# An index beyond the table for edges outside a step's block, and a bound on every row gather of a graph network

## The reference

```python
def gatv2_layer(x, src, dst, Wl, bl, Wr, br, att, bias):
    xl = x @ Wl + bl
    xr = x @ Wr + br
    xj = xl[src]                                   # gather one row per edge
    e = leaky_relu(xj + xr[dst], 0.2)
    logits = e @ att
    ex = exp(logits - segment_max(logits, dst)[dst])
    alpha = ex / (segment_sum(ex, dst)[dst] + 1e-16)
    return segment_sum(alpha[:, None] * xj, dst) + bias
```

## Time and profile before

| | us |
|---|---|
| two runs of the kernel | 12,944.22 and 12,955.25, median 12,949.74 |
| span of the profiled execution, first to last instruction | 12,943.7 |
| pass E0, first to last gather | 218.2 to 2346.9 |
| pass E1 | 2449.5 to 4561.3 |
| layer 1's scatters | 4729.7 to 7807.8 |
| pass E2 | 8067.2 to 10181.7 |
| pass E3 | 10512.2 to 12723.2 |

### The profile page before, as it was taken

How to read it: one execution, slowest core, us unless ns; L and a number is a source line. 1 busy time by engine, 2 the same in 40 slices (tenths; PEclk the granted TensorE clock), 3 DMA queues, 4 the chain that set the end, 5 groups by cost and what they waited for, 6 DMA issues and landing times.

```text
span 12943.7 us, 281524 instructions
## 1 busy us (share of the span) xinstructions
PE 10725.3 (83%) x62317; PEld 8649.8 (67%) x62317; DVE 7913.5 (61%) x29130; ACT 5610.6 (43%) x14105; POOL 9352.2 (72%) x8593
## 2 busy tenths in 40 slices
PE   5788887788888878888888886999999878888886
PEld 4666666666666666666666665777777656666664
DVE  7666666666666655555555555333333568888887
ACT  1555555455555553333333335344444543333334
POOL 3777777577777758888888885777777447777775
PEclk7999999899999966666666667555555688889887
DMA  3222222422222224444444445222222222222222
GB/s 96 56 55 55 55 55 55 132 65 56 56 56 56 55 42 39 39 39 39 39 39 39 38 39 131 57 56 56 56 56 56 58 65 62 62 61 63 61 61 61
DMA packets 809108, 749.26 MB, mean 58 GB/s; under 512 B 264686, under 2 KB 691175, under 8 KB 808255
## 3 DMA queue, kind: packets, MB, share of 16 engines
q0 software_dynamic: 453440, 550.05, 24.5%
q1 hardware_dynamic: 354814, 191.38, 5.7%
HBM read 548.62 MB, written 192.13 MB: 57 GB/s over the span
## 4 chain that ended last, share of the span: by engine, by line
PE 52%; issue 9%; DVE 8%; DMA 6%; POOL 2%; ACT 2%; DVEq 2%; SPq 0%; POOLq 0%; ACTq 0%
PE bank L721 13%; PE bank L705 7%; PE bank L708 6%; DMA scatter_s<-dst_side 6%; PE bank L706 5%; PE bank L1181 4%; PE bank L1187 3%; PE bank L730 3%; PE bank L690 2%; PE bank L1196 2%; POOL scatter_s L1148 2%; DVE agg L929 1%; DVE dst_side L1274 1%; DVE lrelu L884 1%; PE bank L1190 1%
## 5 line engine op out<-in xcount | busy, mean ns | idle before, releaser
L1148 POOL DMA_INDIRECT scatter_s<-dst_side x1664 | 2566.9, 1543 | 555.4 <-DMA scatter_s<-dst_side 240.1
L808 ACT ACTIVATE oh_e<-bank,weight,minus_w 128x128 f32<-128x128 f32 x4992 | 1876.2, 456 | 1465.3 <-PE bank L730 1385.3
L920 DVE SCALAR_TENSOR_TENSOR agg<-agg,rescale,bank 128x130 f32 x4992 | 1680.8, 337 | 1211.0 <-PE bank L721 958.6
L706 PE MATMUL bank<-rows,ident 128*128 128x128 f32 x9984 | 2108.6, 296 | 0.0
L672 POOL DMA_INDIRECT rows<-gather_c,edge_sb x1664 | 1631.9, 981 | 599.6 <-issue 382.3
L672 POOL DMA_INDIRECT rows<-gather_b,edge_sb x1664 | 1605.9, 965 | 608.5 <-issue 314.8
L672 POOL DMA_INDIRECT rows<-gather_a,edge_sb x1664 | 1622.8, 975 | 555.4 <-issue 315.5
L672 POOL DMA_INDIRECT rows<-gather_s,edge_sb x1664 | 1570.3, 944 | 571.3 <-issue 378.7
L721 PE MATMUL bank<-rows,oh_e 128*128 128x130 f32 x9984 | 1873.4, 343 | 54.1 <-DVE agg L920 37.1
L721 PEld LDWEIGHTS bank<-rows,oh_e 128*128 128x128 f32 x9984 | 1601.6, 242 | 268.5 <-issue 230.4
L706 PEld LDWEIGHTS bank<-rows,ident 128*128 128x128 f32 x9984 | 1695.0, 213 | 0.0
(11 more groups left out here) (345 smaller groups left out, 19310.3 us busy)
## 6 DMA issues: line engine op xcount, KB each, us to landing
rows<-gather_a,edge_sb POOLq DMA_INDIRECT x1664
rows<-gather_b,edge_sb POOLq DMA_INDIRECT x1664
scatter_s<-dst_side POOLq DMA_INDIRECT x1664, 3.4
rows<-gather_s,edge_sb POOLq DMA_INDIRECT x1664
rows<-gather_c,edge_sb POOLq DMA_INDIRECT x1664
rows<-scatter_s SPq DMA_DIRECT2D x56, 455.0 KB, 6.1
scatter_s<-zeros SPq DMA_DIRECT2D x64, 390.0 KB, 5.7
edge_sb<-edge_tab SPq DMA_DIRECT2D x520, 40.0 KB
```

Of the source, the lines that this page charges most:

```text
L706: e.matmul(o, ident[:, :], rows[:, it.slot(), g, 0:P], start=False, stop=True).then_inc(L.side.sem, 1)
L808: e.activation(oh_e[:, g % 8, :], bank[7][:, (g % CH) * P:(g % CH + 1) * P], ACT.Relu, bias=weight[:, it.slot(2, 2), g:g + 1], scale=minus ...
L920: e.scalar_tensor_tensor(old, old, rescale[:, it.slot(2, 2), g:g + 1], sum_bank(g)[:, (g % 2) * AW:(g % 2) * AW + L.aw], ALU.mult, ALU.add ...
L1148: e.indirect_dma_start(scatter_s[k], bass.IndirectOffsetOnAxis(ap=S_.target[:, it.slot(1), g:g + 1], axis=0), S_.summed[:, g % 8, :], None ...
```

## The change

In the preparation, part(0) is no longer a copy of the source index. It is computed last, from the mask and the float index: where the mask is -1e30, 2^24 is added to the index. All four gather passes hand each gather a bound of NB * P - 1 = 12,543 in a register; a row whose index is above the bound is not fetched, and its partition keeps what was in it. So that the first use of each slot holds no arbitrary bits, the first pass also sets the 128 columns of all rows to zero before it opens.

```diff
+OUTSIDE = float(1 << 24)
...
 def dve_prep_tile(e, c):
...
             w.wait_ge(tile_turned.at(c))
-            own.did(e.tensor_copy(part(0).bitcast(I32), ps(1)))
             own.did(e.tensor_copy(part(1), ps(0)))
...
             w.wait_ge(own.so_far())
-            e.tensor_tensor(part(2), part(2), mt, ALU.add).then_inc(edges_made.sem, 1)
+            own.did(e.tensor_tensor(part(2), part(2), mt, ALU.add))
+            w.wait_ge(own.so_far())
+            e.scalar_tensor_tensor(part(0).bitcast(I32), part(2), -OUTSIDE / -NEG, part(3), ALU.mult, ALU.add).then_inc(edges_made.sem, 1)
...
 def pool_edges(e, L):
...
                         e.indirect_dma_start(rows[:, u, g, 0:L.width], None, L.src_rows,
-                                             bass.IndirectOffsetOnAxis(ap=edge_sb[:, u, g:g + 1].bitcast(I32), axis=0)
-                                             ).then_inc(L.gat[c].sem(it), 16)
+                                             bass.IndirectOffsetOnAxis(ap=edge_sb[:, u, g:g + 1].bitcast(I32), axis=0),
+                                             bounds_check=NB * P - 1, oob_is_err=False).then_inc(L.gat[c].sem(it), 16)
...
 def dve_edges(e, L):
...
             e.memset(rows[:, :, :, P:XW], 1.0)
+            if L.first:
+                e.memset(rows[:, :, :, 0:P], 0.0)
...
+        E0.first = True
```

More of the change, by code:

```diff
@@ L624, in __init__ @@
                 self.masked = one("masked")
-                self.zeroing, self.zeroed = [], None
+                self.zeroing, self.zeroed, self.first = [], None, False
             def w_last(self, it, lag, c):
```

## The result

The changed kernel takes 13,385.4 us (median of 13,412.93 and 13,357.87) against 12,949.74: a ratio of 1.0338, 95% interval 1.0319 to 1.0358. The forecast was 13,067 us, +0.9%. The sign was right, the size was off by a factor of nearly four (436 us against 117), and the time lies inside the range. The profiled execution is the one of 13,412.93 us, with a span of 13,409.9 us; 466.2 us more than the span before.

What follows compares the result with a forecast made beforehand. POOL's gather issue was taken to bound E0 and E1, nearly E2 and E3. Onto 12,949.74 us came 99.8 (E0, E1), 11 (E2), 0 (E3), 5.2 (memset) and 1.4 (preparation): 117, giving 13,067 us; range 12,770 to 14,100.

Steps and rivals of the forecast that it cites:

- What bounds the kernel: First two gather passes (E0, E1): bound by POOL's back-to-back issue; the other two (E2, E3) nearly so.
- The slack of E2, 39 us: Third gather pass: POOL's waits for PE would absorb 39 of 49.9 us, leaving 11 us.
- that of E3, 73 us: Fourth gather pass: POOL's waits on the chain through VectorE would absorb all 49.9 us, leaving 0.
- The skip saves nothing on the path: All gather passes: skipping 12,416 of 212,992 rows saves nothing in transfers; rival with skip saved: 12,773 us, chance 0.14.
- The end of the bounds at 92 us a pass: POOL's gathers: most the skip could save, if all of 0.944 us scaled with rows.
- I take x = +0.03 us: Every gather on POOL: bound's price net of the skip, chosen between -0.055 and +0.598 us; forecast's chance 0.36.
- row-by-row rival: POOL, all four passes: check paid per row, 1.2 ns each, x = 0.15, 13,843 us; chance 0.32.
- unless a gather itself takes longer: POOL's timeline in the first gather pass: starts 1.25 us apart (0.944 + 0.306), with this one exception.
- The small terms: First pass's memset, 6.9 us with 1.7 covered: +5.2 us; preparation's extra wait, 13 times 0.11 us: 1.4 us.
- The granted clock: Rival on TensorE: slower POOL idles PE, clock falls for half of three passes, 13,940 us; chance 0.08.
- the estimate of 1.28 us per gather: POOL's check at about 12 cycles per element, 1.2 GHz: some 21,400 us in all; no chance given.
- the forecast of 12,957 us: All gathers: bound costs nothing, only +7 us of small terms remains; rival "nothing moves", chance 0.10.

Runs made afterwards that it cites:

- c3: Changed kernel without the bound, no index outside the table, each gather fetching 64 rows instead of 128: 15,217.67 us, single run, against 15,201.85 for the kernel before.
- a3: Changed kernel with the bound set to 0, so nearly every row is skipped: 15,141.35 us, single run, 0.6% over the kernel before.
- b4: Changed kernel with the bound on the third gather pass (E2) alone and no index outside the table: 13,020.07 us, 1.0048 of the kernel before.
- b1: The changed kernel again, unedited, on a chip like the first: 13,429.66 us, 1.0364 of the kernel before.
- a1: Changed kernel with the bound on all gathers but every index inside the table, so no row is skipped: 15,304.99 us against 15,054.77, 1.0156.
- c4: Changed kernel with the bound, no index outside the table, each gather fetching 64 rows instead of 128: 15,262.52 us, single run, against 15,201.85 for the kernel before.
- b2: Changed kernel without the VectorE multiplication by att (L888): 13,106.56 us, 1.0116 of the kernel before.
- b3: Kernel before the change, without the VectorE multiplication by att: 12,839.76 us, 0.9912 of the kernel before.
- a4: Changed kernel with the VectorE multiplication by att (L888) replaced by one with a constant, one SBUF input: 15,265.9 us, 1.0134 of the kernel before.
- c1: Kernel before the change, with the leaky relu's maximum kept in PSUM and multiplied by att from there: 0.9974 of the kernel before.
- a2: Changed kernel without the bound and with no index outside, leaving the memset and the later index: 15,068.54 us, 1.0013 of the kernel before.

## Why the prediction was right in sign and wrong in size

- **What bounds the kernel.** Right. E0 and E1 grew by what their gathers grew, 140.3 and 148.0 us of busy time for 140.6 and 148.4 us of pass. The slack of E2, 39 us, was 37.8; that of E3, 73 us, gave only 43.4, and 30 us of waits stayed. The forecast counts all slack as cover, 112 us; 81 were.
- **The skip saves nothing on the path.** The forecast took it as nothing; that held more strictly than argued. The end of the bounds at 92 us a pass was far out: even rows that are left out altogether save 0.7 ns each (c3), and skipped ones save none (a3; b4 against b1).
- **The failed step: "I take x = +0.03 us".** The bound costs 0.053 us on every gather (a1, b4), 353 us in all where the forecast had 200, before slack. I placed x by the zero between rows of 512 and 516 bytes, and the width of a row turned out to say nothing about a check. With 0.053 the sum would have been 6656 x 0.053 - 112 + 7 = 248 us, within 2% by a hair. This part is the mechanism of the forecast with a mis-sized term. The row-by-row rival has the sign but not the form: about half of the 53 ns is paid per gather (c4).
- **The term that was missing.** The forecast takes the median for the length of a gather ("unless a gather itself takes longer") and gives the long gathers no term. 193 us come from them: they last up to 0.8 us longer, and there are more of them. They were in the profile: a maximum of 1,762 ns beside a median of 944 in E0, and 1,067 in E2, a mean 31 ns over the median in one and none in the other. I read over it. Without L888 the changed kernel loses 267 us and not 467 (b2, b3). The Trainium skill has the rule, on its page SBUF — State Buffer, section "SBUF: two separate sides": VectorE, in a fast mode that uses both of its ports or, against a GpSimd operation that reads SBUF, with two SBUF inputs, and GpSimd exclude each other on a shared pair of ports. The trace agrees on which instructions: L888 (two SBUF inputs) lengthens gathers, and so does its stand-in of a4, which has one but gets through the same elements in 407 ns instead of 673; the form with a PSUM operand does not (c1). The page also has whichever starts first hold the pair for its whole instruction. There the trace differs: L888 often starts after the gather, and it is the gather that waits.
- **Why there are more of them.** Why the changed kernel meets L888 more often, 252 gathers of E0 against 115, is only argued: gathers and VectorE run at the pace of the same turn, and a longer gather shifts one against the other. On the other kind of chip there is no such rise (175 with the bound in a1, 190 without it in a2), so the 193 us are this kernel's on this kind of chip and no fixed price of the bound. How much they would grow no row of the kernel before shows.
- **The small terms.** The memset took 6.88 us (6.9 forecast) and opened the pass 8.3 us later (5.2 + 1.4 forecast); with the index it is 14 us in a2, between 3 and 35.
- **Other rivals.** The granted clock did fall, from 0.94 and 0.93 to 0.90 and 0.89, but PE has idle time there and the passes grew only by their gathers, so it cost nothing. The prediction says that E2's low clock goes with a PE short of work; by its own rows PE is busy there for 286.5 us of 300 at 0.50, so busy time does not show it. The Trainium skill, page GPSIMD Engine Reference, section "3.1 Elementwise — side-by-side cycle accounting", gives 12 cycles per element for a data-dependent branch. This check does not cost that: the estimate of 1.28 us per gather worked out from it stands against 0.053 measured. The Trainium skill's page DMA: Bandwidth & Descriptors, section "Anatomy of one DMA — SWDGE (gpsimd) path", calls descriptor generation "small, variable". The bound's 53 ns are small beside a gather's 0.944 us, but the forecast of 12,957 us drawn from that word does not hold: on 6,656 gathers, mostly issued back to back, they come to 353 us.

## What to carry to other kernels

Where an engine issues its DMAs back to back, the unit to count is the instruction and not the row or the byte. Here 53 ns on a distance of 1.25 us are 4%, and E0 grew by 4% where no long gathers hid it (91 us on 2,080, b2 against b3). A skip that leaves the number of DMAs as it is saves nothing there. Compare maximum and mean of a duration with its median before taking the median for the price: here the spread came from a second engine in the way, and it grew with a shift of pace. To save on outside rows here, whole gathers would have to go.

## What the runs showed of the hardware beyond that

- An indirect gather of 128 rows holds POOL for 0.944 us and one of 64 rows for 0.899, then 0.30 us pass to the next. By a straight line through the two this is 0.7 ns per row on a fixed 0.85 us, an estimate.
- A bound on the index adds 53 ns (39 with 64 rows), whether rows are skipped or not. A skipped row moves 4 bytes instead of 512. A gather has 32 packets in every run, with 128 or 64 rows and with rows skipped or not.
- A VectorE instruction with two SBUF inputs made a gather last up to 0.8 us longer when it ran about 0.1 us after the gather's start, and not when it started 0.3 us or more after it (0 of 179). The instruction itself was never longer. The faster one-input form of a4 also did it when it started 0.5 to 0.8 us after (69 of 90). One with a PSUM operand (5 of 212 in c1) and the reduction (0 of 88) hardly or never did.
- The same program takes 12,950 us on some chips and 15,055 to 15,202 us on others, with the same median of a gather without a bound, 0.944 or 0.947 us. In a2 all of the difference lies in the four gather passes, 460 to 630 us each, mostly as idle time of POOL, with "remote" as a frequent releaser; the granted clock in E0 is 0.81 there instead of 0.94. Which is cause and which effect was not found.
